# Two quarters of the attention probabilities transposed by DMA, row sums from a column of ones, masked maximum in five passes

## What is computed

```python
# layer 0: mean over the neighbours, two linear maps, relu, residual, layer norm
mask = adj > 0
agg  = mask @ x / max(sum(mask, 1), 1)
x    = layernorm(x + relu(concat(x @ W_self + b_self, agg @ W_nb + b_nb) @ W_comb + b_comb))
# layer 1: masked attention on hidden size 32, values of 128 columns
x_att = tanh(x @ Wx1 + bx1) @ Wx2 + bx2            # 4096 x 32
n_att = tanh(neigh @ Wn1 + bn1) @ Wn2 + bn2        # 4096 x 32
ws    = softmax(where(adj > 0, leaky_relu(x_att @ n_att.T), -9e15), axis=1)
out   = concat(x @ Wfx + bfx, ws @ (neigh @ Wv + bv))
x     = layernorm(x + out)
```

## Time and profile before

| what | value |
|---|---|
| runs | 731.31, 731.82, 731.85 us |
| profiled execution, own time | 732.47 us |
| its span, first to last instruction | 730.6 us |
| granted TensorE clock, mean | 0.993 of full speed |
| PE, PEld, DVE, ACT, POOL busy, share of the span | 95, 81, 85, 80, 16% |
| chain that ended last | PE 86%, ACT 5%, DVE 4% |

### The profile page before, as it was taken

The page is one execution under the profiler, slowest core; times in us unless marked ns, Lnnn a source line. Parts: engine busy times, 40 slices in busy tenths (PEclk is TensorE's granted clock), DMA queues, the critical chain, the costliest instruction groups (busy, mean ns, idle before and its releaser), DMA issues.

```text
span 730.6 us, 20042 instructions
## 1 busy us (share of the span) xinstructions
PE 690.8 (95%) x7344; PEld 592.1 (81%) x7344; DVE 623.3 (85%) x1567; ACT 584.1 (80%) x1048; POOL 116.1 (16%) x241
## 2 busy tenths in 40 slices
PE   5989998999999999999999999999999999998775
PEld 4646676888888888888888888888888888886554
DVE  4887668999999999999999999999999999987874
ACT  2455248888888888888888988888888888889885
POOL 0010111111111111111111111111111111111201
PEclk9989999999999999999999999999999999999999
DMA  8966999999999999999999999999999999841111
GB/s 269 371 146 162 228 283 220 189 204 234 195 191 211 222 207 208 210 225 210 225 205 209 215 197 218 187 193 234 204 199 218 211 219 224 168 68 35 37 47 44
DMA packets 260147, 141.40 MB, mean 194 GB/s; under 512 B 225361, under 2 KB 243665, under 8 KB 260049
## 3 DMA queue, kind: packets, MB, share of 16 engines
q1 hardware_dynamic: 259604, 140.10, 88.0%
q10 hardware_dynamic: 444, 0.02, 0.0%
HBM read 81.35 MB, written 4.19 MB: 117 GB/s over the span
## 4 chain that ended last, share of the span: by engine, by line
PE 86%; ACT 5%; DVE 4%; issue 3%; POOL 1%; DMA 1%; SPq 0%; ACTq 0%; POOLq 0%; DVEq 0%
PE ps_v L1137 21%; PE ps_agg L1093 15%; PE ps_agg L1096 14%; PE ps_t L1117 11%; PE ps_s L1108 7%; PE ps_agg L1156 3%; PE ps_agg L1159 3%; PE ps_s L1007 2%; PE ps_v L1015 2%; ACT score L915 2%; PE ps_t L998 1%; PE ps_x L1176 1%; PE ps_x L1179 1%; PE ps_x L1024 1%; PE ps_agg L1147 1%
## 5 line engine op out<-in xcount | busy, mean ns | idle before, releaser
L1093 PE MATMUL ps_agg<-x,mask_t 128*128 128x257 f16 x1024 | 243.2, 273 | 0.0
L1096 PE MATMUL ps_agg<-x,mask_t 128*128 128x256 f16 x1024 | 237.3, 273 | 0.3 <-DVE x L527 0.3
L908 ACT ACTIVATE score<-ps_s,sc 128x512 f32<-128x512 f32 x256 | 178.5, 697 | 55.7 <-PE ps_s L1108 51.9
L686 DVE CUSTOM_DVE_ANT_0 score<-score,mask 128x512 f32<-128x512 f32 x256 | 176.0, 687 | 13.3 <-ACT score L908 13.1
L1137 PEld LDWEIGHTS ps_v<-v,late 128*128 128x128 f16 x2304 | 143.3, 97 | 39.0 <-DVE late L750 16.7
L1137 PE MATMUL ps_v<-v,late 128*128 128x128 f16 x2304 | 160.1, 219 | 10.8 <-DVE late L750 5.9
L915 ACT ACTIVATE score<-score,exp_bias,sc 128x1024 f32<-128x1024 f32 x128 | 159.3, 1245 | 3.2 <-DVE exp_bias L695 3.2
L750 DVE TENSOR_TENSOR late<-ps_t,late 128x512 f16<-128x512 f32 x192 | 131.3, 684 | 31.9 <-ACT late L922 30.5
L922 ACT CAST late<-ps_t 128x512 f16<-128x512 f32 x192 | 114.4, 596 | 19.2 <-PE ps_t L1117 19.2
L1117 PE MATMUL ps_t<-ident,score 128*128 128x128 f32 x768 | 118.4, 277 | 7.3 <-ACT score L915 7.3
L1096 PEld LDWEIGHTS ps_agg<-x,mask_t 128*128 128x128 fp8e4 x1024 | 100.2, 98 | 15.6 <-issue 5.2
(11 more groups left out here) (134 smaller groups left out, 822.0 us busy)
## 6 DMA issues: line engine op xcount, KB each, us to landing
adj_sb<-in_adj_dram SPq DMA_DIRECT2D x128, 512.0 KB, 5.4
neigh_sb<-in_L_gnn_neigh_dram SPq DMA_DIRECT2D x8, 512.0 KB, 7.9
score<-in_x_dram SPq DMA_DIRECT2D x8, 512.0 KB, 8.5
x_in<-in_x_dram SPq DMA_DIRECT2D x32, 128.0 KB, 2.6
out_dram<-out_sb SPq DMA_DIRECT2D x32, 128.0 KB, 3.4
mask_t<-mask SPq DMA_TRANSPOSE x128, 4.7
neigh_sb<-neigh_sb SPq DMA_TRANSPOSE x64, 3.7
mask<-in_L_gnn_W_comb_dram SPq DMA_DIRECT2D x1, 512.0 KB, 8.5
```

What stands on the lines that cost most here:

```text
L686: dve.tensor_tensor_reduce(score[:, b % 2, part], score[:, b % 2, part], mask[:, b % MASK_BUFS, part], 1.0, -3.0e38, ALU.subtract, ALU.max ...
L908: act.activation(score[:, b % 2, k * GW:(k + 1) * GW], ps_s[k % 2][:, :], ACT.Prelu, alpha=SLOPE, scale=score_scale).then_inc(leaky_made, 1)
L1093: mm = pe.matmul(agg[:, 0:D + 1], mask_t8[:, c, 0, :], x16[:, c, X_HI:X_ONE + 1], start=(c == 0), stop=(c == NC - 1), skip_group_check=True)
L1096: mm = pe.matmul(agg[:, 0:D], mask_t8[:, c, 0, :], x16[:, c, X_LO:X_LO + D], start=False, stop=False, skip_group_check=True)
```

## The change

Quarters 0 and 1 of the probabilities are now both split first and transposed by DMA, each on its own semaphores and with its own buffers; only quarters 2 and 3 go over PE (16 transposes per block in place of 24). The exponentials run in the order 0, 1, 2, 3 and no longer sum; the sum comes from a column of ones beside the values, so the matmuls with the high values have 129 columns. The masked maximum takes 1024 columns in three passes and 512 in two. Where the steps stand now: `wide_high` slots 33 and 35, `wide_low` 34 and 36, `turn_wide` 35 and 37 (at the head of SP's slot, before the masks), `turn_p` 35 to 38, `p_low` and `p_high` with it, `weigh_values` 36 to 39 for PE's quarters, 40 and 41 for quarter 0, 42 and 43 for quarter 1. `layer1` (with the reciprocal and its scaling) 44, in slot 4; its statistics in a step of their own at 46, in slot 6, after `layer0` and before the stack; POOL's `norm2` 46, `normalise2` 47. The slots end four later.

```diff
+VW = 2 * DV + 2
+V_ONE, V_LO = DV, DV + 2
+MASKED = ((0, 2), (2, 4), (4, 6), (6, 7), (7, 8))
-TURN_AT = 33
-WEIGH_AT = 34
+TURN_AT = 35
+WEIGH_AT = 36
-BY_PE = NG - BY_DMA
-EXPS = ((0, 1), (1, 0), (2, 2), (4, 3))
-WIDE_HIGH_AT = 35
-WIDE_LOW_AT = 36
-WIDE_TURN_AT = 37
-LAYER1_AT = 42
+BY_PE = NG - 2 * BY_DMA
+EXPS = ((0, 0), (1, 1), (2, 2), (4, 3))
+WIDE_HIGH_AT = (33, 35)
+WIDE_LOW_AT = (34, 36)
+WIDE_TURN_AT = (35, 37)
+WIDE_WEIGH_AT = (40, 42)
+LAYER1_AT = 44
+NORM2_AT = 46
...
+            def turn_wide(b, w):
+                sp.wait_ge(wide_lo_made[w], b + 1)
                 at_least(sp, pv_done, NG * b)
+                for half in range(2):
+                    sp.dma_start_transpose(wide_t[:, w, half, :, :], wide_p[:, w, half, :]).then_inc(wide_t_in[w], 16)
...
+            pool.memset(v16[:, :, V_ONE:V_LO], 1.0).then_inc(consts_ready, 1)
...
+            def masked_scores(b, j):
+                first, end = MASKED[j]
+                dve.wait_ge(leaky_made, NG * b + end)
+                dve.wait_ge(mask_made, NQ * b + (end + 1) // 2)
+                part = slice(first * GW, end * GW)
...
-            def row_scale(b):
...
             def layer1(b):
+                base = 5 * b
                 right = res[:, b % RES_BUFS, DV:D]
                 dve.wait_ge(pv_done, NG * (b + 1))
                 dve.wait_ge(res_made, b + 1)
+                dve.reciprocal(row2[:, 1:2], ps_v[:, V_ONE:V_ONE + 1]).then_inc(l1_step, 1)
+                dve.wait_ge(l1_step, base + 1)
+                dve.tensor_scalar(row2[:, 2:3], row2[:, 1:2], v_inv, None, ALU.mult).then_inc(l1_step, 1)
+                dve.wait_ge(l1_step, base + 2)
                 dve.scalar_tensor_tensor(out=right, in0=ps_v[:, 0:DV], scalar=row2[:, 2:3], in1=right,
                                          op0=ALU.mult, op1=ALU.add).then_inc(l1_step, 1)
+            def layer1_statistics(b):
+                base = 5 * b
+                dve.wait_ge(l1_step, base + 3)
+                dve.bn_stats(stat2[:, :], res[:, b % RES_BUFS, :]).then_inc(l1_step, 1)
+                dve.wait_ge(l1_step, base + 4)
...
-                act.activation(part, part, ACT.Exp, bias=exp_bias[:, b % 2:b % 2 + 1], scale=score_unit,
-                               accum_out=sums[:, b % 2, q:q + 1]).then_inc(exp_made, 1)
+                act.activation(part, part, ACT.Exp, bias=exp_bias[:, b % 2:b % 2 + 1],
+                               scale=score_unit).then_inc(exp_made, 1)
...
+                    for part, (p, v, n) in enumerate(((hi, 0, DV + 1), (hi, V_LO, DV), (lo, 0, DV + 1))):
+                        mm = pe.matmul(ps_v[:, 0:n], p, v16[:, c, v:v + n],
```

More of the change, by code:

```diff
@@ L300, in gnn_kernel @@
         p_hi_made = sem("p_hi_made")
-        wide_hi_made = sem("wide_hi_made")
-        wide_lo_made = sem("wide_lo_made")
-        wide_t_in = sem("wide_t_in")
+        wide_hi_made = [sem(f"wide_hi_made{w}") for w in range(BY_DMA)]
+        wide_lo_made = [sem(f"wide_lo_made{w}") for w in range(BY_DMA)]
+        wide_t_in = [sem(f"wide_t_in{w}") for w in range(BY_DMA)]
         x1_hi_made = sem("x1_hi_made")
@@ L405, in _ @@
             for s in range(0, SLOTS + 3):
+                for w, at in enumerate(WIDE_TURN_AT):
+                    if d := due(s, at, 0):
+                        turn_wide(d[0], w)
                 for q, at in enumerate(MASK_SLOTS):
@@ L518, in v_low @@
                 dve.wait_ge(v_hi_made, turn + 1)
-                dve.scalar_tensor_tensor(out=v16[:, part, DV:2 * DV],
+                dve.scalar_tensor_tensor(out=v16[:, part, V_LO:VW],
                                          in0=ps_s[turn % 2][:, :].rearrange("p (u n) -> p u n", u=TR), scalar=v_scale,
@@ L751, in p_low, with wide_low @@
                                   ALU.subtract).then_inc(p_lo_made, 1)
[L753 to L756, removed]
-            def row_scale(b):
[L759 to L765, removed]
+            def wide_low(b, w):
+                dve.wait_ge(wide_hi_made[w], b + 1)
+                dve.tensor_tensor(wide_p[:, w, 1, :], score[:, b % 2, w * QW:(w + 1) * QW], wide_p[:, w, 0, :],
+                                  ALU.subtract).then_inc(wide_lo_made[w], 1)
             def layer1(b):
-                base = 6 * b
+                base = 5 * b
                 right = res[:, b % RES_BUFS, DV:D]
@@ L784, in _ @@
                     layer1(d[0])
-                if d := due(s, SCORE_AT + 1):
-                    masked_scores(*d)
+                for j, (_, end) in enumerate(MASKED):
+                    if d := due(s, SCORE_AT + end, 0):
+                        masked_scores(d[0], j)
                 if d := due(s, MEAN_AT, 0):
@@ L800, in _ @@
                     layer0(d[0])
+                if d := due(s, NORM2_AT, 0):
+                    layer1_statistics(d[0])
                 if d := due(s, STACK_AT, 0):
@@ L806, in _ @@
                         make_mask(d[0], q)
-                if d := due(s, WIDE_LOW_AT, 0):
-                    wide_low(d[0])
+                for w, at in enumerate(WIDE_LOW_AT):
+                    if d := due(s, at, 0):
+                        wide_low(d[0], w)
                 if d := turned_by_pe(s, TURN_AT):
@@ L975, in _ @@
                         exps(d[0], q)
-                if d := due(s, WIDE_HIGH_AT, 0):
-                    wide_high(d[0])
+                for w, at in enumerate(WIDE_HIGH_AT):
+                    if d := due(s, at, 0):
+                        wide_high(d[0], w)
                 if d := turned_by_pe(s, TURN_AT):
@@ L1204, in _ @@
                     scores(*d)
-                if d := due(s, WEIGH_AT):
-                    weigh_values(*d)
+                if d := turned_by_pe(s, WEIGH_AT):
+                    weigh_values(*d[0:2])
+                for w, at in enumerate(WIDE_WEIGH_AT):
+                    if (d := due(s, at)) and d[1] < 2:
+                        weigh_values(d[0], BY_PE + 2 * w + d[1])
 _INS = ['x', 'adj', 'L0_gnn_W_self', 'L0_gnn_b_self', 'L0_gnn_W_nb', 'L0_gnn_b_nb', 'L0_gnn_W_comb', 'L0_gnn_b_comb',
```

88 lines of the change are left out of this document (35 added, 53 removed).

## The result

The changed kernel takes 762.27 us (median of four runs, 759.06 to 764.35); the kernel before took 731.57 us beside it (four runs, 731.31 to 731.85). The ratio is 1.0411, 95% interval 1.0395 to 1.0428: slower, 2 us above the forecast of 760 and inside the range. The profiled execution took 761.88 us, its span is 760.1.

A forecast was written before the change was run, and what follows sets the result against it. A loop through PE, DVE and ACT was taken to bound the kernel, beside nearly full PE: 0.93 us more per period, 25.1 over 27, plus 3.0 in the way out, gives 760 us, range 740 to 772.

The forecast's parts named there:

- The loop: Cycle through PE, DVE and ACT between quarter-2 exponentials: period from 19.54 to 20.47 us; chance 0.81, slower.
- stretch 1: From the quarter-2 exponential to DVE's masked maximum of slot 5, by way of PE: stays 8.14 us.
- ACT's stretch: From the next block's first exponential to its quarter 2 on ACT: 5.25 us becomes 5.35.
- DVE's side of stretch 1: DVE's own way to the slot 5 masked pass: start at 1.85 plus 6.29 of work, 8.14 us, in time.
- the upper bound of 20.62: Period in us if a masked pass of 1024 columns takes 1.38 us, as two old passes do.
- stretch 2: DVE alone, from the slot 5 masked pass to the end of row_max: 5.83 us becomes 6.95.
- Nothing, while these slots cover it.: Two more DMA transpositions per block cost nothing: landing takes 3.7 us, PE uses quarters five slots, over 12 us, after issue.
- The rival that named the DMA engines: Full DMA engines set the time: 13% more bytes, 22.1 us per period, about 803 us; chance 0.04.
- 0.93 more per period, 25.1 over 27.: Added time in us between quarter-2 exponentials, per period and over the 27 periods of blocks 0 to 27.
- I charge nothing: PE's granted clock stays at full speed, 2.4 GHz, despite some 1.8 us of idling per period: no cost.
- The way out: After the quarter-2 exponential of block 27: 3.0 us more in all, bounds 0 and 6.
- the very end: Four more slots, reciprocal and scaling on the last path, last input transposed by DMA: 1.6 us more.

The follow-up runs named there:

- Experiment 1: Kernel before with only the 1024-column masked passes and layer 1's statistics moved to slot 6; 750.67 us, ratio 1.0257.
- experiment 4: Changed kernel, only high halves transposed by DMA after block 0: 759.29 us; the same with the exponential of quarter 2 first: 747.27 us.
- experiment 6: Single 2048-column DMAs: changed kernel with quarter 2 first, 757.53 us; kernel before plus one spare quarter copy, 748.20, or two, 836.13. Packet time counted too.
- experiment 2: Changed kernel with the statistics of layer 1 back in slot 4 in place of slot 6; 758.28 us, ratio 1.0359.

## Why the prediction was right, and where it was not

**The loop.** Right in every term of the sum: stretch 1 8.05 (8.14 forecast), row_max at +14.96 (15.09), the first exponential at +15.00 (15.12), ACT's stretch 5.40 (5.35), the pass of 1024 columns 1.22 (1.23), `wide_high` 383.53 to 384.47, 0.94. `layer1` in slot 4 was indeed covered: DVE still waited 0.47 us behind it for `leaky`. PE's idle time, 1.42 us per period, was put at 1.8. Experiment 1 shows the DVE terms alone, experiment 4 that the added transfers are not needed for 20.40. Two workings beside the sum were off, without effect here. DVE's side of stretch 1 came to 7.58 (8.05 less the wait of 0.47), not 8.14: the 5.67 us taken over from the kernel before held 0.41 + 0.15 us of waits for ACT, and both are gone. And the upper bound of 20.62 lets a pass of 1.38 lengthen stretch 2 alone; by the forecast's own sum it lengthens DVE's side of stretch 1 by another 0.15.

**"Nothing, while these slots cover it."** In the changed kernel this held: PE waited for no transposed quarter. But there was less room than the forecast thought, which set five slots, over 12 us, against a landing of 3.7. Quarter 1 of the period above (its low half is done on DVE at 371.98, 370.75 + 1.23):

```profile
376.56 3.72 SPq L380 DMA_TRANSPOSE neigh_sb<-neigh_sb  x2
...
384.81 0.85 PE L1148 MATMUL ps_v<-v,neigh_sb 128*128 128x129 f16 x12
```

SP came to it 4.6 us late, behind quarter 0, a mask, a load and `x1`; the second DMA landed at 383.97, and PE used it 0.8 us later (2.4 us in the mean of blocks 2 to 26). What failed is the ground on which the DMAs were put at nothing; the total came out all the same, by luck, because the loop stands a little above the floor that was left out. The rival that named the DMA engines was put aside with "single microseconds have a share of 0.06, so the queue runs empty". That row was misread. The view counts a packet with its whole duration in the slice where it starts, as the slice before it shows in the kernel before:

```profile
345.00:346.00 1.00, 1.00 (x16) 0.85 (x15) 0.94 (x5) 0.47 (x2) 0.27 (x1) 1.00 2.60 232
```

A share of 2.60 is followed by 0.06; the packets of the one slice were still running in the other. Idle time existed, 36 of 400 us in all, but that is 9%, and the change adds some 2.0 us to 17.8, 11%. Nor was 22.1 us, that rival's price, right: it scaled the period with the bytes as if the engines had been full before. With 17.77 + 2.04 it would have read 19.8, and the measured kernels stand at 20.2 to 20.4.

**"0.93 more per period, 25.1 over 27."** The sum is met (25.25), but by luck and not by equal parts: 26 intervals got 0.86, the first one 2.91. PE of the changed kernel in that first one (start, duration):

```profile
119.47 1.12 PE L1127 MATMUL ps_t<-ident,score 128*128 128x128 f32 x4 [2.65 <-ACT score L924]
120.38 0.42 PE L1106 MATMUL ps_agg<-x,mask_t 128*128 128x256 f16 x1
```

The same stretch in the views by stretch (the PE clock is the third figure from the end), then the changed kernel of experiment 4 at the same place, its whole first interval first:

```profile
119.47:124.00 4.53, 4.53 (x26) 3.81 (x27) 2.83 (x5) 1.95 (x3) 0.00 (x0) 0.50 1.25 285
...
118.09:137.62 19.53, 18.22 (x201) 15.89 (x201) 16.48 (x34) 16.13 (x26) 1.78 (x4) 1.00 1.09 226
...
119.40 0.66 PE L1127 MATMUL ps_t<-ident,score 128*128 128x128 f32 x4 [2.65 <-ACT score L924]
```

In the changed kernel PE waited 2.65 us and then ran four transposes in 1.12 us instead of 0.66 and a matmul in 0.42 instead of 0.27, with a granted clock of 0.50 (1.2 GHz) from 119.47 to 124 us; the interval's mean is 0.85. In experiment 4 the changed kernel had the same wait of 2.65 us, the clock stayed at 1.00 and the interval was 19.53, as long as one before. So "I charge nothing" for the clock was wrong in this execution and would have been right in that one.

**The way out.** Forecast 3.0, measured 4.76. The interval to block 28 got 1.00 (0.9 forecast), the next three 0.15 + 0.22 + 0.34 (0.5), the very end 3.05 where 1.6 had been put: that is the term that was mis-sized. With fewer transfers, in experiment 4, the end is 1.34 us shorter. The very end, before and after:

```profile
714.25:730.57 16.32, 8.43 (x115) 6.99 (x112) 7.55 (x16) 7.20 (x13) 2.11 (x6) 0.91 0.19 50
740.69:760.05 19.36, 11.18 (x124) 10.33 (x124) 7.53 (x16) 6.64 (x10) 2.11 (x6) 0.75 0.29 69
```

PE is busy 2.75 us longer there, at a lower granted clock, which the forecast of the end had not charged either; how much of the 3.05 the clock makes was not tried apart.

## What to carry to other kernels

Where engines run a written order, close the loop through their waits and write its length beside each engine's work: an edit that takes work from the fullest engine gains nothing if it lengthens the loop, and here 0.85 us taken from PE was bought with 0.9 us of loop and some 2 us of DMA. Write down every floor, the DMA engines' too, before trading one for another, and test a cause by removing it and by removing its rival: opening the loop alone gained nothing (0.9 us), halving the transfers alone hardly more (3.0, within the scatter of the runs), both together 15 us. A DMA share of one slice of a microsecond says little; count the idle time over a long stretch.

## What the hardware showed that had not been expected

**Transposing DMAs.** The Trainium skill (Perfetto Trace Analysis, Identifying the Most-Contended Engine) judges the DMAs by HBM utilization first, not by occupancy, and then asks which DMA resource binds. By the first step they look no worse after the change: the profile before has 117 GB/s over the span and the one after this row:

```profile
HBM read 81.35 MB, written 4.19 MB: 113 GB/s over the span
```

The transposed quarters go from SBUF to SBUF, and the time with a packet under way went from 364 to 399 us of 400; here the first step misses what the measurement shows, and the measurement decides. The Trainium skill (DMA: Bandwidth & Descriptors, Latency and other measured facts) gives 261 GB/s as the effective rate of a transposing DMA with a non-contiguous middle dimension; as an estimate from that page, 512 KB would take 2.0 us. The count in experiment 6 is near that, with 1.9 to 2.1; whether the transfers here are of that kind, no run shows.

**The clock.** At the same wait of 2.65 us of PE the granted clock fell to 0.50 in one execution and stayed at 1.00 in another. The four runs of the changed kernel scatter in the order of their mean granted clock: 759.06 us at 0.990, 761.88 at 0.985, 762.66 and 764.35 at 0.982; the kernel before, where PE idles 0.6 us between 118 and 646 us, took 731.31 to 731.85. That the clock makes the scatter is likely, not tested.

**POOL beside DVE.** A masked pass of 512 columns took 1.09 to 1.12 us instead of 0.68 in 28 blocks of experiment 2, where it began some 0.15 us after POOL had begun to add the biases, and 1.12 in the one block of the changed kernel where it did so (at 133.67 us). In the kernel before the same two overlap in 28 blocks with the pass begun 0.35 us before POOL, and each of these took 0.68. So the order in which they begin goes with the difference; why was not tested.
